# Second GEMM of blocks 1 to 7: units 4 to 6 as seven half-size products, unit 7 added in PSUM

## The chip, the cores and the metric

The kernel runs on one core of a Trainium2 chip. The metric is the device time of one execution in microseconds (us); of several runs the median is given. Trace times count from the span's start. TensorE is PE, VectorE DVE, ScalarE ACT, GpSimd POOL and SyncE SP.

## The reference, cut to what matters

`x` is (4, 1024, 1024). A gate with two decaying scans over the sequence (forward and backward) makes the input of a feed-forward layer, whose result is added to `x`:

```python
num = nf + nb - ekv + euk * vf
den = df + db - ek + euk
base = jax.nn.sigmoid(r) * (num / jnp.maximum(den, 1e-08))
out = base * (0.8 + 0.2 * tf)
...
h = jnp.einsum('bsd,fd->bsf', out, W1)              # W1: 4096 x 1024
q = jnp.clip(jnp.round(h / 0.1), -2**15, 2**15 - 1)
a = jax.nn.gelu(q * 0.1)
x = x + jnp.einsum('bsf,df->bsd', a, W2)            # W2: 1024 x 4096
```

The weights are ternary times powers of two. The kernel checks that they fit its short form (`bad`, the "checks") and has a general path behind a flag, which does not run here.

## The kernel before, in words

The sequence is cut into 8 blocks of 512 positions (`T`), two for each batch entry. For each block 8 tiles of 128 channels are made by the scans (`part`, `newton`, `mixed_out` on DVE; `tile_group` on ACT, exponentials and logarithms). While block n is in the two GEMMs, the tiles of block n+1 are made: `mix(t, p)` is step p of tile t (0 weigh, 1 forward, 2 backward, 3 sums). Where block n+1 is the first half of its batch entry, each tile also needs a prefix over the other half ("late" tiles: two more exponentials on ACT, two more products on DVE). That is so while blocks 1, 3 and 5 are in the GEMMs. Block 7 has no tiles beside it.

Values are split into a high and a low f16 half, and each matmul is done for both. The first GEMM of blocks 1 to 7 has 8 units of 512 hidden channels. Each is done by the seven-product scheme for a 2 x 2 matrix of quadrants: seven products of half the size in both directions instead of eight (`products_15`, `products_73`, `products_26`, `product_4`, L831 to L866), each 16 matmuls of 256 columns, with sums of operands made beforehand (`convert`) and sums of results made in PSUM: `seed` copies product 1 on ACT, `spill_p5` saves product 5 on ACT, `seed_u4` adds on DVE, `quantise22` finishes the fourth quadrant on DVE. The quantised unit goes through GELU on ACT (`gelu`).

In the second GEMM units 0 to 3 are done by the same scheme: `quad_sums` and `quads_lo_*` on DVE and `quads_hi_*` on ACT make the seven operands of a unit, and two output parts e = 0, 1 of four output tiles follow (`y_15_begin`, `y_15_end`, `y_26`, `y_15`, `y_73`, `y_4`, L868 to L929), 32 matmuls of 256 columns for each product. Their quadrants are written out by `y_quad` (ACT) and `y22` (DVE) and added to the output in DRAM by POOL's accumulating DMAs. Units 4 to 7 are done plainly: `act_hi` (ACT) and `act_lo` (DVE) make two halves, and `output` (L947) adds 32 matmuls of 512 columns for each of the 8 output tiles; `output_out` (ACT) empties them. They lie at the end of a block. The last tile of the last block is done in two halves (`output_end`), read back from the output, added and stored (`residual_end`, `result_end`, `store_end`).

The order on each engine is written by hand, block by block: `chained_block` on ACT (L1320) and DVE (L1943), `ffn_block` on SP (L589), the loop at L987 on PE. Every engine works strictly in that order and waits on semaphores. Weights come through a ring of 8 slots filled by SP (`ring_load`, L468); a slot is loaded again when the product that read it is done. A check loads a piece of weights (`load_check`, SP), rounds it to 8 bits (`check_i8`, ACT) and compares (`check`, DVE), with one buffer; a block has eight of them, the last block sixteen. An activation table is loaded whenever ACT changes from exponentials to GELU and back (`tile_group_between`, L1124).

Of the kernel before, what the change touches and what calls it, by code (L numbers as in the profile page):

```python
# [5 lines left out]
P = 128  # L6
# [13 lines left out]
MIX_SCALE = 4.0  # L20
# [18 lines left out]
def adaln_ffn_kernel(nc, x, fside, cond, w, u, w1, w2, out):  # L39
# [18 lines left out]
    CHAIN = STEPS + 2  # L58
# [3 lines left out]
    with ExitStack() as ctx:  # L62
# [11 lines left out]
        w2s = nc.dram_tensor("w2s", [2, P, 4, 2, KH2 * P], F16).ap()  # L74
        w1_quads = w1_half.rearrange("s p (h f k q) -> s p h f k q", h=2, f=2, k=2)
# [5 lines left out]
        wy_ring = w_ring[:, :, :].rearrange("p s (i g m) -> p s i g m", i=2, g=KH2)  # L81
        w_gen = w_ring[:, :, :].bitcast(F32).rearrange("p (s a) n -> p s (a n)", s=2)
# [5 lines left out]
        ao = act_flat[:, 0:SPLIT * 7 * 2 * T].rearrange("p (s o j a t) -> p s o j a t", s=SPLIT, o=7, j=2, a=2)  # L88
# [36 lines left out]
        chk_full = tt_flat[:, 2 * T:4 * T]  # L125
# [6 lines left out]
        chk_i8 = q16[:, 1, 0, :].bitcast(I8)  # L132
        end_full = m_st[:, 0, :, :].rearrange("p k t -> p (k t)")
        end_i8 = m_st[:, 2, 0, 0:T // 2].bitcast(I8)
# [34 lines left out]
        y_end = [halves[7][:, 0, :], halves[2][:, 1, :]]  # L169
# [83 lines left out]
        s_chkload = sem("s_chkload")  # L253
# [12 lines left out]
        s_ev = sem("s_ev")  # L266
        s_yend = sem("s_yend")
        s_resend = sem("s_resend")
# [21 lines left out]
        def part_y(n, e):  # L290

            return CHAIN * (n - 1) + SPLIT + 1 + e

        def emptied(q, c):

            m, r = q // CHAIN, q % CHAIN
            if r in (SPLIT + 1, SPLIT + 2):
                return (s_y11, s_y12, s_y21)[c], 2 * m + r - SPLIT
            return (s_q11, s_q12, s_q21)[c], STEPS * m + (r if r <= SPLIT else r - 2) + 1

        def lo_half(n, s, h):

            return 2 * s + h if n == 0 else 2 * STEPS + 2 * (STEPS - SPLIT) * (n - 1) + 2 * (s - SPLIT) + h

        def quad_unit(n, s):

            return SPLIT * (n - 1) + s

        def act_at(n, s):

            if n == 0:
                return FPS * s
            return FT - FPS if s == SPLIT else FPS * (s - SPLIT - 1)

        def q_at(s, k, h):

            return q_quads[:, s % 2, k, h, :, :] if s < SPLIT else q16[:, s % 2, 2 * k:2 * k + 2, H * h:H * h + H]

        def ao_two(s, o, p):

            return ao[:, s, o:o + 2, :, p, :].rearrange("p o j t -> p (o j) t")

        def w1_pair(s, h):

            return (s // 2 + 2 * h, s % 2) if s < SPLIT else (s, h)
# [7 lines left out]
        def quad(dram, e, c):  # L333

            return dram[4 * e + c // 2:4 * e + 4:2, :, H * (c % 2):H * (c % 2 + 1)].rearrange("i p t -> p i t")

        def event(e, c):

            return ((0, 0), (0, 3), (0, 1), (1, 0), (0, 2), (1, 3), (1, 1), (1, 2)).index((e, c))
# [5 lines left out]
        def buffer_free(engine, n, i):  # L345

            if added(n, i) > 0:
                engine.wait_ge(s_acc[i % 4], 16 * added(n, i))
            elif i % 4 < 2:
                engine.wait_ge(s_res[i % 4], DT // 2)  # L350
            else:
                engine.wait_ge(s_store[i % 4 - 2], 16 * DT // 2)
# [7 lines left out]
        def check_buffers(at):  # L360

            return (chk_full, chk_i8) if at < END_CHECKS else (end_full, end_i8)
# [12 lines left out]
        def y_all(n, d):  # L375

            return y_half(d, 1) if n == 0 else 2 * DT + DT * (n - 1) + d + 1
# [4 lines left out]
        def ring_chunks():  # L382
# [13 lines left out]
            ready_y = [(s_w2store[k], 16 * 4) for k in range(2)]  # L396
            for n in range(1, BLOCKS):
# [14 lines left out]
                def plain(e, r, u, done):  # L412
                    return (w2_half[4 * e + r:4 * e + 4:2, :, u * KH2 * P:(u + 1) * KH2 * P].rearrange("i p n -> p i n"), SLOT,
                            [], [(done, part_y(n, e) + 1)])

                def summed(e, form, done):
                    return (w2s[e][:, form, :, :], SLOT, ready_y if n == 1 and e == 0 and form == 0 else [],
                            [(done, part_y(n, e) + 1)])

# [30 lines left out]
                yield w2_part(0, 1), SLOT, [], [(s_y, y_all(n, 0))]  # L450
                yield h73(LAST)
                yield w2_part(1, 1), SLOT, [], [(s_y, y_all(n, 1))]
                yield h4(LAST)
                for d in range(2, DT):
                    yield w2_part(d, 1), SLOT, [], [(s_y, y_all(n, d))]
# [4 lines left out]
        def _(sp):  # L460
# [7 lines left out]
            def ring_load(times=1):  # L468
                for _ in range(times):
# [45 lines left out]
            def residual_end(n, d):  # L515

                for k in range(4):
                    sp.wait_ge(s_acc[k], 16 * added(n, 8))
                sp.wait_ge(s_acc[1], 16 * (added(n, 2 * DT - 3) + 1))
                sp.dma_start(x_in[:, 1, :], out[n // 2, 1 - n % 2, d]).then_inc(s_x[1], 16)  # L520

            def store_end(n, d):
                sp.wait_ge(s_resend, 1)
                sp.dma_start(out[n // 2, 1 - n % 2, d][:, 0:H], y_out[:, 1, 0:H]).then_inc(s_store[1], 16)
                sp.wait_ge(s_res[1], uses_of(n, d) + 1)
# [1671 lines left out]
```

## Time and profile before

| | us |
|---|---|
| median of 3 runs (1728.91 to 1730.32) | 1729.12 |
| the profiled execution | 1728.37 |
| its span | 1726.6 |
| PE busy | 1648.9 (96%) |
| DVE busy | 1232.5 (71%) |
| ACT busy | 986.4 (57%) |
| POOL busy | 139.2 (8%) |
| mean granted TensorE clock | 0.990 |

Busy times are sums of instructions, and the share is of the span. An instruction can start before the one ahead of it on its engine has ended, so the distance of two starts (the pitch) is often shorter than a duration. In the list of instructions each line has its start, its length, engine, line of the kernel, operation, the tile written and the tiles read, and in brackets the idle time before it with what ended it.

### The profile page before, as it was taken

The numbers are of one execution on the slowest core, as the hardware profiler recorded it, in microseconds if no ns is written. First come the engines' busy times: TensorE is split into PE (matmuls) and PEld (weight loads), VectorE is DVE, ScalarE is ACT, GpSimd is POOL, SyncE is SP. The second block draws the span as 40 slices with busy tenths as digits, with TensorE's granted clock in tenths as the row PEclk, the third lists the DMA queues.
The fourth block names the chain that finished last, engine by engine and source line by source line (L and its number), as shares of the span: only waits on it lengthen the run. The fifth ranks groups of instructions, "written<-read, shape, count | busy, mean of one in ns | idle before, by whom it ended". The sixth has DMA issues, their size and how long they took to land. (4 is left out here: it accounts for less than half of the span.)

```text
span 1726.6 us, 30636 instructions
## 1 busy us (share of the span) xinstructions
PE 1648.9 (96%) x12258; PEld 1199.1 (69%) x12258; DVE 1232.5 (71%) x1684; ACT 986.4 (57%) x1558; POOL 139.2 (8%) x155
## 2 busy tenths in 40 slices
PE   1699999999999999999999999999999999999996
PEld 0234445888578884888658885688847887488863
DVE  8888797878768658687677767786886875854131
ACT  4577423765666565674747656476666647465341
POOL 0000110011000101002010010001010010100101
PEclk9799999999999999999999999999999999999998
DMA  8979895688575866769386684868757694676754
GB/s 237 237 183 275 276 333 172 218 254 220 127 244 188 252 177 183 237 200 262 122 218 236 214 232 127 235 215 248 226 137 217 204 247 151 175 243 200 195 185 98
DMA packets 131205, 362.54 MB, mean 210 GB/s; under 512 B 14000, under 2 KB 28592, under 8 KB 130096
## 3 DMA queue, kind: packets, MB, share of 16 engines
q1 hardware_dynamic: 105216, 308.33, 52.8%
q0 software_dynamic: 25840, 52.18, 17.8%
q8 instruction: 99, 1.62, 0.4%
q14 instruction: 50, 0.41, 0.1%
HBM read 333.19 MB, written 81.79 MB: 240 GB/s over the span
## 5 line engine op out<-in xcount | busy, mean ns | idle before, releaser
L813 PE MATMUL ps<-mo,w_ring 128*128 128x256 f16 x6272 | 695.1, 273 | 5.1 <-DVE q L1758 2.7
L813 PEld LDWEIGHTS ps<-mo,w_ring 128*128 128x128 f16 x6272 | 613.1, 98 | 82.5 <-issue 7.1
L957 PE MATMUL ps<-act,w_ring 128*128 128x512 f16 x1760 | 383.3, 379 | 0.0
L876 PE MATMUL ps<-act,w_ring 128*128 128x256 f16 x3136 | 348.1, 273 | 0.7
L876 PEld LDWEIGHTS ps<-act,w_ring 128*128 128x128 f16 x3136 | 305.8, 98 | 38.4 <-issue 2.5
L957 PEld LDWEIGHTS ps<-act,w_ring 128*128 128x128 f16 x1760 | 172.2, 98 | 203.2
L1784 DVE SCALAR_TENSOR_TENSOR act<-a,act 128x1024 f16<-128x1024 f32 x72 | 87.8, 1222 | 91.3 <-ACT act L1233 91.3
L1223 ACT ACTIVATE a<-q 128x1024 f32<-128x1024 int16 x124 | 131.0, 1057 | 7.0 <-DVE act L1784 2.0
L724 POOL DMA_DIRECT2D out_dram<-xy x56 | 66.9, 1195 | 810.6 <-ACT xy L1257 709.6
L1746 DVE SCALAR_TENSOR_TENSOR ps<-sp,ps 128x512 f32<-128x512 f32 x70 | 48.4, 692 | 110.2 <-issue 49.4
L754 PE MATMUL ps<-mo,w_ring 128*128 128x512 f16 x256 | 66.7, 424 | 56.8 <-DMA w_ring<-w_half 34.9
L943 PE MATMUL ps<-act,w_ring 128*128 128x512 f16 x512 | 110.7, 379 | 0.0
L1273 ACT ACTIVATE q<-tt 128x1024 int8<-128x1024 f32 x48 | 50.4, 1049 | 77.0 <-DMA tt<-in_w_dram 77.0
L754 PEld LDWEIGHTS ps<-mo,w_ring 128*128 128x128 f16 x256 | 26.5, 107 | 96.4 <-issue 47.4
L943 PEld LDWEIGHTS ps<-act,w_ring 128*128 128x128 f16 x512 | 50.1, 98 | 60.4
L729 POOL DMA_DIRECT2D out_dram<-xy x55 | 47.6, 883 | 544.1 <-ACT xy L1264 539.0
L1257 ACT ACTIVATE xy<-ps 128x512 f32<-128x512 f32 x42 | 24.7, 588 | 112.0 <-PE ps L876 112.0
L1648 DVE SCALAR_TENSOR_TENSOR ND<-EE,bonus,ND 128x1024 f32<-128x1024 f32 x64 | 81.9, 1280 | 2.9
L1845 DVE SCALAR_TENSOR_TENSOR tt<-q,tt 128x1024 f32<-128x1024 int8 x48 | 58.6, 1221 | 35.0 <-ACT q L1273 34.9
L1628 DVE TENSOR_TENSOR_SCAN ND<-decay,back,ND 128x512 f32<-128x512 f32 x64 | 81.9, 1280 | 0.6
L1632 DVE TENSOR_TENSOR_SCAN ND<-decay,back,ND 128x512 f32<-128x512 f32 x64 | 81.6, 1276 | 0.0
L1172 ACT ACTIVATE ps<-ps 128x512 f32<-128x512 f32 x70 | 40.8, 582 | 68.4 <-PE ps L813 38.2
(132 smaller groups left out, 1812.0 us busy)
## 6 DMA issues: line engine op xcount, KB each, us to landing
w_ring<-w1s SPq DMA_DIRECT2D x168, 512.0 KB, 5.7
w_ring<-w_half SPq DMA_DIRECT2D x130, 512.0 KB, 5.5
w_ring<-w2s SPq DMA_DIRECT2D x56, 512.0 KB, 5.1
out_dram<-xy POOLq DMA_DIRECT2D x111, 256.0 KB, 6.2
tt<-in_w_dram SPq DMA_DIRECT2D x48, 512.0 KB, 5.3
V<-in_fside_dram SPq DMA_DIRECT2D x64, 256.0 KB, 5.6
R<-in_x_dram SPq DMA_DIRECT2D x64, 256.0 KB, 5.9
w_half<-in_w_dram POOLq DMA_DIRECT2D x16, 1024.0 KB, 10.3
```

Of the source, the lines that this page charges most:

```text
L724: pool.dma_start(quad(dram, e, c), xy_quads[:, k, :, :], accum_op=ALU.add).then_inc(s_acc[k], 16)
L754: mm = pe.matmul(bank[4 * (s % 2) + j][:, :], w1_ring[:, slots[2 * s + j // 2], j % 2, c, :], mix0[:, c, p, :], start=(first and p == 0), ...
L813: mm = pe.matmul(dst[:, f, :], wp_ring[:, k, r, f, q, :], mo[:, op, q, p, :], start=(fresh and f == 0 and q == 0 and p == 0), stop=(q == K ...
L876: mm = pe.matmul(dst[:, i, :], wy_ring[:, k, i, 2 * s + j, :], ao[:, s, op, j, p, :], start=(fresh and i == 0 and s == 0 and j == 0 and p ...
L943: mm = pe.matmul(y_ps[y][:, :], w2_ring[:, k, f, :], act[:, FPS * s + j, p, :], start=(h == 0 and f == 0 and p == 0), stop=(h == 1 and f = ...
L957: mm = pe.matmul(bank[d][:, :], w2_ring[:, k, FPS * (s - SPLIT) + j, :], act[:, act_at(n, s) + j, p, :], start=(s == SPLIT and j == 0 and ...
L1223: sc.activation(a32[:, 2 * h:2 * h + 2, :], src[:, s % 2, 2 * h:2 * h + 2, :], ACT.Gelu_apprx_tanh, scale=QSTEP).then_inc(s_gelu, 1)
L1628: v.tensor_tensor_scan(DEN[:, k, :][:, ::-1], dec(b, c), DEN[:, k, :][:, ::-1], back[:, k, 1:2], ALU.mult, ALU.add).then_inc(s_dbwd, 1)
L1632: v.tensor_tensor_scan(NUM[:, k, :][:, ::-1], dec(b, c), NUM[:, k, :][:, ::-1], back[:, k, 0:1], ALU.mult, ALU.add).then_inc(s_nbwd, 1)
L1648: v.scalar_tensor_tensor(out=ND[:, k, :, :], in0=EE[:, k, :, :], scalar=bonus[:, b, c:c + 1], in1=ND[:, k, :, :], op0=ALU.mult, op1=ALU.ad ...
L1784: v.scalar_tensor_tensor(out=act[:, f:f + 2, 1, :], in0=a32[:, 2 * h:2 * h + 2, :], scalar=ACT_SCALE, in1=act[:, f:f + 2, 0, :], op0=ALU.m ...
L1845: v.scalar_tensor_tensor(out=full, in0=small, scalar=1.0 / W_SCALE, in1=full, op0=ALU.mult, op1=ALU.not_equal, accum_out=bad[:, at:at + 1] ...
```

## The change

Units 4 to 6 also go through the seven-product scheme in the second GEMM, as two further output parts e = 2, 3, with 24 matmuls of 256 columns for each product. Unit 7 keeps its two plain halves and is added to the quadrants of these parts in PSUM by `z_product`: 16 matmuls of 256 columns for each quadrant; the fourth quadrant goes on top of product 5 in its bank, which is then spilled again (`spill_z`). `output`, `output_out` and `output_end` go. The operands of units 4 to 6 take the place of operands that are done with (`operand_at`).

The weight sums for the new products (`w2f`) are made in block 1: `f_load` and `f_store` are DMAs issued by ACT, `f_sums` is on DVE. POOL copies unit 7's weights together once (`w2z`). The weights of the new parts come in 14 pieces of 384 KB and two of 512 KB for each block where eight of 512 KB came.

The checks have two buffers at each place and their loads are issued by ACT (`check_load`, `next_check`) and not by SP. The output's last quadrant is read back early into a buffer of its own.

The diff is long; this is its core. First the new functions and the order on PE:

```diff
+            def z_product(n, k, dst, c):
+
+                r, h = c // 2, c % 2
+                for i in range(2):
+                    for j in range(FPS):
+                        pe.wait_ge(s_alo, lo_half(n, LAST, j // 2) + 1)
+                        for p in range(2):
+                            mm = pe.matmul(dst[:, i, :], wz_ring[:, k, 2 * i + r, j, :],
+                                           act[:, act_at(n, LAST) + j, p, h * H:(h + 1) * H],
+                                           start=False, stop=(j == FPS - 1 and p == 1), skip_group_check=True)
+                return mm
...
+                begun = y_15_begin(n, 2)
                 products_73(n, LAST)
...
+                y_15_end(n, 2, begun)
+                y_26(n, 2)
                 product_4(n, LAST)
...
+                y_15(n, 3)
+                y_73(n, 2)
+                held = loaded()
+                z_22(n, 2, held)
+                z_11(n, 2, held)
+                z_12(n, 2, held)
+                y_26(n, 3)
+                y_4_end(n, 2, held)
+                held = loaded()
+                z_22(n, 3, held)
+                y_73(n, 3)
+                z_11(n, 3, held)
+                z_12(n, 3, held)
+                y_4_end(n, 3, held)
...
+            def spill_z(n, e):
+
+                q = part_y(n, e)
+                act_e.wait_ge(s_z22, 2 * (n - 1) + e - 1)
+                act_e.wait_ge(s_u4, q + 1)
+                act_e.wait_ge(s_sp5, q + 1)
+                sc.activation(sp5[:, q % 2, :], bank[4 * (q % 2) + 2][:, :], ACT.Copy, scale=1.0 / MIX_SCALE).then_inc(s_zsp, 1)
...
+            def f_load(k):
+
+                if k == 0:
+                    block_done(act_e, 0)
+                else:
+                    act_e.wait_ge(s_fsum, 4 * k)
...
+            def check_load(at):
+
                 if at > 0:
...
+                    act_e.wait_ge(s_chk, at - 1)
...
+                act_e.dma_start(check_buffers(at)[0], check_rows(at)).then_inc(s_chkload[at % 2], 16)
+
+            def next_check(*ats):
+
+                for at in ats:
+                    if at % DT in (1, 2, 5, 6) if at < END_CHECKS else END_CHECKS < at < 2 * STEPS * FPS - 1:
+                        check_load(at + 1)
+                    check_i8(at)
...
+            def f_sums(k):
+
+                dve.wait_ge(s_fload, 32 * (k + 1))
...
+                upper, lower = f_in[:, 0, :, :], f_in[:, 1, :, :]
+                v.tensor_tensor(f_out[:, 0, :], lower[:, 0, :], lower[:, 1, :], ALU.add).then_inc(s_fsum, 1)
```

The order on ACT from unit 6's product 5 on, and in block 1 (lines taken out are left away):

```diff
+                    if n == 1 and s > 2:
+                        f_store(s - 3)
+                        f_load(s - 2)
...
                 seed(hid(n, SPLIT + 2))
                 spill_p5(hid(n, SPLIT + 2))
                 if nxt:
                     tile_group(g0 + 5)
+                    next_check(at + 3)
+                    check_load(at + 4)
+                    check_load(at + 5)
...
                 quantise12(n, SPLIT + 1)
                 gelu(n, SPLIT + 1, 0)
                 quantise11(n, SPLIT + 2)
...
+                quads_hi_11(n, SPLIT + 1)
                 quantise21(n, SPLIT + 1)
                 gelu(n, SPLIT + 1, 1)
                 seed(hid(n, LAST))
...
+                quads_hi_2(n, SPLIT + 1)
                 spill_p5(hid(n, LAST))
...
+                quads_hi_t(n, SPLIT + 1)
+                if nxt:
+                    tile_group_between(g0 + 6)
+                else:
+                    next_check(at + 10)
                 quantise12(n, SPLIT + 2)
                 gelu(n, SPLIT + 2, 0)
                 quantise11(n, LAST)
...
+                quads_hi_11(n, SPLIT + 2)
                 quantise21(n, SPLIT + 2)
                 gelu(n, SPLIT + 2, 1)
...
+                quads_hi_2(n, SPLIT + 2)
+                quads_hi_t(n, SPLIT + 2)
+                quantise12(n, LAST)
+                seed(part_y(n, 2))
```

The order on DVE from output part 0 on (likewise):

```diff
+                if n == 1:
+                    f_sums(3)
                 seed_u4(part_y(n, 0))
                 mix(2, 0, 1)
...
+                quads(SPLIT)
                 mix(2, 2)
...
+                y22(n, 0)
                 mix(2, 3)
...
                 mix(3, 0, 1)
...
+                seed_u4(part_y(n, 1))
+                mix(3, 2, 3)
+                check(at if nxt else at + 7)
+                mix(4, 0)
+                y22(n, 1)
+                if nxt:
+                    check(at + 1)
+                mix(4, 1, 2)
+                seed_u4(hid(n, SPLIT + 1))
+                mix(4, 3)
+                if nxt:
+                    check(at + 2)
+                mix(5, 0, 1)
+                quantise22(n, SPLIT + 1)
+                check(at + 3 if nxt else at + 8)
+                mix(5, 2)
+                seed_u4(hid(n, SPLIT + 2))
+                mix(5, 3)
+                quads(SPLIT + 1)
                 quantise22(n, SPLIT + 2)
...
+                mix(6, 0)
                 seed_u4(hid(n, LAST))
...
+                quads(SPLIT + 2)
+                mix(6, 1)
+                quantise22(n, LAST)
+                mix(6, 2)
+                act_lo(n, LAST, 0)
+                check(at + 4 if nxt else at + 11)
+                seed_u4(part_y(n, 2))
+                mix(6, 3)
+                act_lo(n, LAST, 1)
...
+                convert(n + 1, 0)
                 mix(7, 0)
...
+                convert(n + 1, 1)
                 mix(7, 1)
...
+                y22(n, 2)
+                mix(7, 2)
+                check(at + 5)
+                seed_u4(part_y(n, 3))
```

## Rows read from the trace of the kernel before

**Rows 1.** The page, part 1: busy time, share of the span, instructions.

```profile
PE 1648.9 (96%) x12258; PEld 1199.1 (69%) x12258; DVE 1232.5 (71%) x1684; ACT 986.4 (57%) x1558; POOL 139.2 (8%) x155
```

**Rows 2.** Five blocks: length, busy PE, PEld, DVE, ACT, POOL (instructions), PEclk, DMA, GB/s.

```profile
289.06:491.30 202.24, 202.13 (x1601) 156.42 (x1600) 155.84 (x217) 126.96 (x201) 15.59 (x15) 1.00 0.70 205
491.30:693.77 202.47, 202.30 (x1602) 156.34 (x1600) 145.71 (x185) 122.76 (x192) 16.14 (x16) 1.00 0.69 204
693.77:898.10 204.33, 202.46 (x1602) 156.25 (x1601) 158.62 (x225) 129.43 (x204) 15.96 (x17) 1.00 0.70 210
898.10:1102.54 204.44, 202.45 (x1601) 156.27 (x1600) 147.38 (x189) 122.77 (x192) 17.31 (x17) 1.00 0.69 203
...
1508.92:1711.40 202.48, 202.37 (x1633) 159.42 (x1631) 71.79 (x104) 91.46 (x117) 15.54 (x16) 1.00 0.64 191
```

**Rows 3.** Instructions of PE in order of time, block 3 (start, length, idle before).

```profile
720.98 3.65 PE L813 MATMUL ps<-mo,w_ring 128*128 128x256 f16 x32 [0.85 <-ACT ps L1172]
725.55 26.36 PE L813 MATMUL ps<-mo,w_ring 128*128 128x256 f16 x240 [0.92 <-DVE q L1758]
...
770.96 24.62 PE L876 MATMUL ps<-act,w_ring 128*128 128x256 f16 x224
...
849.75 48.51 PE L957 MATMUL ps<-act,w_ring 128*128 128x512 f16 x224
```

**Rows 4.** DMA issues by line: KB each, median us from issue to landing.

```profile
tt<-in_w_dram SPq DMA_DIRECT2D x48, 512.0 KB, 5.3
```

**Rows 5.** Instructions in order of time at the span's end, PE and DVE.

```profile
1704.26 7.15 PE L973 MATMUL ps<-act,w_ring 128*128 128x256 f16 x64
...
1719.93 0.42 DVE L1833 SCALAR_TENSOR_TENSOR xy<-ps,xy 128x256 f32<-128x256 f32 x1 [8.20 <-DMA xy<-out_dram]
```

**Rows 6.** Instructions of DVE in order of time, block 3.

```profile
727.59 0.68 DVE L1573 SCALAR_TENSOR_TENSOR EE<-EKP,EE 128x512 f32<-128x512 f32 x1
...
737.46 1.28 DVE L1608 TENSOR_TENSOR_SCAN ND<-decay,pre_n,EE 128x512 f32<-128x512 f32 x1
...
740.54 0.69 DVE L1746 SCALAR_TENSOR_TENSOR ps<-sp,ps 128x512 f32<-128x512 f32 x1
741.44 1.23 DVE L1795 TENSOR_TENSOR tt<-a 128x1024 f32<-128x1024 f32 x1 [0.21 <-ACT a L1223]
...
748.64 1.28 DVE L1628 TENSOR_TENSOR_SCAN ND<-decay,back,ND 128x512 f32<-128x512 f32 x1
...
752.33 0.69 DVE L1746 SCALAR_TENSOR_TENSOR ps<-sp,ps 128x512 f32<-128x512 f32 x1
...
780.25 1.22 DVE L1845 SCALAR_TENSOR_TENSOR tt<-q,tt 128x1024 f32<-128x1024 int8 x1
...
781.39 1.28 DVE L1648 SCALAR_TENSOR_TENSOR ND<-EE,bonus,ND 128x1024 f32<-128x1024 f32 x1
...
783.32 0.68 DVE L1767 SCALAR_TENSOR_TENSOR xy<-ps,sp 128x512 f32<-128x512 f32 x1
```

**Rows 7.** Instructions of ACT in order of time, a tile group of block 3.

```profile
840.60 1.28 ACT L1126 ACT_TABLE_LOAD   x1
...
843.04 0.71 ACT L1095 ACTIVATE EE<-RAMP,lndec 128x512 f32<-128x512 f32 x1
...
846.89 1.28 ACT L1223 ACT_TABLE_LOAD   x1
```

**Rows 8.** Instructions of DVE in order of time, block 1 (it starts at 289.06).

```profile
322.41 0.69 DVE L1746 SCALAR_TENSOR_TENSOR ps<-sp,ps 128x512 f32<-128x512 f32 x1
```

**Rows 9.** Instructions of SP's queue in order of time, two issues in block 3.

```profile
769.88 0.41 SPq L536 DMA_DIRECT2D tt<-in_w_dram  x1
770.34 0.43 SPq L490 DMA_DIRECT2D VP<-in_fside_dram  x1
```

**Rows 10.** Instructions of PE in order of time, block 0.

```profile
71.29 23.77 PE L754 MATMUL ps<-mo,w_ring 128*128 128x512 f16 x96 [6.28 <-DVE mo L1675]
```

**Rows 11.** Busy time by stretch, block 0 (columns as in rows 2).

```profile
71.00:83.00 12.00, 11.71 (x41) 4.74 (x42) 11.18 (x17) 8.14 (x17) 0.49 (x1) 0.74 0.80 198
```

More of the change, by code:

```diff
@@ L252, in adaln_ffn_kernel @@
         s_store = [sem(f"s_store{k}") for k in range(2)]
-        s_chkload = sem("s_chkload")
+        s_chkload = [sem(f"s_chkload{k}") for k in range(2)]
         s_chki8 = sem("s_chki8")
@@ L265, in adaln_ffn_kernel @@
         s_acc = [sem(f"s_acc{k}") for k in range(4)]
-        s_ev = sem("s_ev")
-        s_yend = sem("s_yend")
-        s_resend = sem("s_resend")
+        s_z22 = sem("s_z22")
+        s_zsp = sem("s_zsp")
+        s_w2z = sem("s_w2z")
+        s_fload = sem("s_fload")
+        s_fsum = sem("s_fsum")
+        s_fstore = [sem(f"s_fstore{k}") for k in range(2)]
         s_vote = sem("s_vote")
@@ L396, in ring_chunks @@
             ready_y = [(s_w2store[k], 16 * 4) for k in range(2)]
+            ready_f = [(s_fstore[k], 16 * 4) for k in range(2)]
             for n in range(1, BLOCKS):
@@ L708, in _ @@
                 pool.dma_start(w2_half[d], w2_full[d]).then_inc(s_w2cast[d], 16)
+            for d in range(DT):
+                pool.wait_ge(s_w2cast[d], 16)
+            for e in range(2):
+                for u in range(2):
+                    rows = w2_half[4 * e:4 * e + 4].rearrange("d p (u n) -> d p u n", u=4)[:, :, 2 + u, KF * P:KH2 * P]
+                    pool.dma_start(w2z[e][:, :, u, :], rows.rearrange("d p n -> p d n")).then_inc(s_w2z, 16)
             for s in range(STEPS):
@@ L1988, in chained_block @@
-                seed_u4(part_y(n, 1))
-                mix(3, 2)
-                mix(3, 3)
-                y22(n, 1)
-                mix(4, 0)
-                mix(4, 1)
-                seed_u4(hid(n, SPLIT + 1))
-                mix(4, 2)
-                if not nxt:
-                    check(at + 5)
-                mix(4, 3)
-                quantise22(n, SPLIT + 1)
-                mix(5, 0)
-                seed_u4(hid(n, SPLIT + 2))
-                act_lo(n, SPLIT + 1, 0)
-                mix(5, 1)
@@ L2048, in chained_block @@
-                if nxt:
-                    convert(n + 1, 3)
-                    check(at + 5)
+                y22(n, 2)
+                mix(7, 2)
+                check(at + 5)
+                seed_u4(part_y(n, 3))
+                mix(7, 3)
+                convert(n + 1, 2)
+                y22(n, 3)
+                divide(g0 + 7)
+                convert(n + 1, 3)
                 if n + 2 < BLOCKS:
```

686 lines of the change are left out of this document (355 added, 331 removed).

## The prediction

> **What bounds the kernel now.** I began with the page's first line and then took the busy times block by block. TensorE is busy 96% of the span [rows 1], and in blocks 1 to 7 it is busy 202.1 to 202.5 us of blocks that last 202.2 to 204.4 us [rows 2]. A matmul that is not waiting is therefore the bound, and the reader should first see what one costs. In block 3, 224 matmuls of 512 columns begin at 849.75 and the block ends 48.35 us later, so one takes 215.8 ns; 224 of 256 columns take 24.46 us (24.62 less the 0.16 by which a line's last matmul outlasts its pitch), so one takes 109.2 ns [rows 3]. The only waits of TensorE in that block are 0.85 us for ScalarE's seed and 0.92 us for VectorE's `quantise22` [rows 3]; they are why blocks 3, 4 and 5 are about 1.8 us longer than the others [rows 2] (block 5 reads like block 3 with 203.9 us, block 6 like block 2 with 202.5; of the seven rows five stand). The second thing to see is what cover is left: VectorE is busy 156 to 159 us in blocks 1, 3 and 5, where the tiles of the next block carry a prefix, about 146 us in blocks 2, 4 and 6, and 72 us in block 7, which has no tiles [rows 2].
>
> **TensorE's own gain.** A block loses 8 x 4 x 4 x 2 = 256 matmuls of 512 columns (55.3 us). It gains 2 x 7 x 24 = 336 of 256 columns for units 4 to 6 and 2 x 4 x 16 = 128 for unit 7, 464 in all (50.7 us). That is 4.6 us a block and 32.2 us in seven, all of it on the path. The last block's 64 half-width matmuls already stand for 32 wide ones, so it saves the same.
>
> **The waits of blocks 3 to 5.** They come from ScalarE sitting on a check's load, of which there was one buffer: a load takes 5.3 us to land [rows 4], and the check before it must be done first. With two buffers the load for the start of a block is issued in the block before or one check ahead. I take the 1.8 us in three blocks as gone, 5.3 us.
>
> **The end.** TensorE's last long line ends at 1711.4 and the span at 1726.6. VectorE waited 8.20 us there for a read-back of the output, and from its result at 1719.93 to the end are 6.7 us [rows 5]. Afterwards the read-back lies early, and the result follows the last matmul at once: 0.1 us, the 6.7, 0.3 for a result of twice the size and up to 3 for a store of twice the bytes, 10.1 us against 15.2, so 5 less. Without any new wait the time would be 1728.4 - 32.2 - 5.3 - 5 = 1685.9 us, taking the profiled execution's own 1728.37 us (span 1726.6; the median of the three runs, 1729.12, lies 0.04% above).
>
> **What the other engines get.** One unit in seven products costs VectorE 6.6 us: from its first sum at 741.44 to the backward scan at 748.64 are 7.2 us, of which 0.6 is a `quantise22` [rows 6]. Two `act_lo` go, of 1024 elements like the check that starts at 780.25, whose pitch is 1.14 us [rows 6]. Three units add 13 us, two `seed_u4` and two `y22` 2.4 us: VectorE comes to 174 us of 197.8 in a late block, 161 in an early one. ScalarE gains about 7 us: four stores instead of two per unit, and two seeds, four spills and six quadrants instead of eight outputs. Neither becomes the bound by its sum. What counts is the order, because the stretch that goes, 48 us of plain matmuls that waited for nobody, was where both engines caught up.
>
> **Late blocks (1, 3, 5), in order of time from the block's start.** Positions of TensorE are counts of matmuls times 109.2 ns. The pieces of VectorE are pitches of rows 6: weigh 2.07 us (three operations of 0.69 from 727.59), forward 3.08 (737.46 to 740.54), backward 3.69 (748.64 to 752.33), check 1.14, sums 1.93 (781.39 to 783.32).
> (a) Unit 5. The spill of unit 6's fifth product can't come before matmul 1104, at 120.5 us. Behind it in ScalarE's order stands the tile group, whose weight is ready 1.87 us after the group's first operation (841.88, behind the table load, to 843.75) [rows 7], so with the spill's 0.6 at 123.0. VectorE must weigh and scan before `quantise22` of unit 5: 123.0 + 2.07 + 3.08 + 0.7 = 128.9. TensorE wants that at matmul 1168, 127.5 us: 1.5 us late.
> (b) Unit 6. Check, backward, seed, sums, seven-product sums and `quantise22`: 128.9 + 1.14 + 3.69 + 0.6 + 1.93 + 6.6 + 0.7 = 143.6. TensorE stands there at 141.4: 2.3 us.
> (c) The fifth product of output part 2 needs unit 6's sums. ScalarE was held until check `at + 3` is done (the load of `at + 5` waits for it) and reaches the tile group at 140.2. A group between two GELUs takes 5.7 us (840.60 to 846.89, less the 0.6 of a quantise) and the way back a table load of 1.28 us [rows 7], so the GELU ends at 151.4, and sums, stores and lower halves take 5.6 us more: 157.0 against 153.1: 3.9 us.
> (d) `y22` of part 2 stands behind two conversions and a scan: 187.6 against 185.9: 1.7 us.
> The four come to 9.4 us. In blocks 3 and 5 the tile group ahead of the block's last quadrant delays the first seed, and the start costs 1.1 us more: 10.5 us.
>
> **Early blocks (2, 4, 6).** Weighing is one operation (0.6 us) and the group lacks two exponentials (1.15 us). (a) and (d) fall within the margin, (b) leaves 0.9 and (c) 2.6 us: 3.5 us.
>
> **Block 1's weight sums.** VectorE gets four times four sums on 128x768 f16, a form no row has; the nearest row, 512 f32 elements, takes 0.69 us [rows 6], and between half of that and all of it I take 0.5, 2 us a group. `seed_u4` of unit 2 ended 0.9 us before TensorE wanted it (322.41 + 0.69 is 34.0 us into the block, and the third product starts at 34.9) [rows 8], so the first group costs about 1.9 us with the issues ahead of it. The second and third wait for loads that ScalarE issues some 45 and 61 us into the block and that land 5.3 us later, behind a VectorE that is ready sooner: 2.9 and 1.6, and 0.5 at unit 3's sums. That is 6.9 us on top of (a) to (d), 16.3 in all. Bounds: 0 if the loads are early, 11 if every issue holds ScalarE.
>
> **Block 7's checks.** Sixteen checks in pairs, each second load issued only when the pair before is done, ahead of `seed_u4`: ScalarE sits on a landing of 5.3 us in units 3 and 4. I get 3.2 and 1.3 us, 1.1 at unit 3's sums and 1.9 at unit 6's: 7.5 us.
>
> **DMAs issued by ScalarE.** Eight check loads a block leave the SP queue for ScalarE's. SP's issues stand 0.46 us apart [rows 9]; whether one holds ScalarE as long, no row shows, so between 0 and 0.46. I take half, since the sequencer can issue beside a running activation of 0.6 to 1 us; it is in the sums above. [...] Loads of tiles and weights stay ahead: the tail's weights grow from 4.2 to 6.6 MB a block at 0.70 busy DMA [rows 2], and eight slots reach some 20 us ahead.
>
> **Sum.** 16.3 + 2 x 10.5 + 3 x 3.5 + 7.5 = 55.3 us of new waits. 1685.9 + 55.3 = 1741.2, so 1741 us. The work saved is real; the waits cost more.
>
> **Rivals.** (B) Faster: the lateness of (a) and (b) isn't there. Both are differences of one to two per cent of 130 us of in-order work, so if VectorE reaches `quantise22` of unit 5 by 127.4 us, (a) and (b) vanish and (c), fed by the same chain, halves: 5.7 us less in each late and 2.2 in each early block, 23.7 in all: 1717 us. For it speaks that VectorE's 174 us leave 23 us in a late block; against it, that the weight exponential is bound to a spill, not to VectorE's load. (C) Slower still: TensorE's clock falls in the longest waits. After a wait of 6.28 us, 96 matmuls took 23.77 us instead of 20.72, and the granted clock over 71 to 83 us was 0.74, between the two levels of 1.2 and 2.4 GHz [rows 10, 11]; after waits of 0.9 us in block 3 the clock stays at 1.00 [rows 2, 3]. Four waits of 3 to 4 us at up to 3.05 us each give 1753. [...] (D) Gains and waits cancel: within 0.2% (3.5 us, about what a measurement of this kernel can tell from no change) of 1729, if 40 to 47 us of waits remain.
>
> **Chances and range.** The forecast 0.46 (its own range 1733 to 1748), B 0.34, C 0.10, D 0.10. Faster is B, 0.34; same is D, 0.10; slower 0.56. From B's lower side, where block 1's and block 7's waits shrink too, to C's upper: 1702 to 1758.
>
> **What would show it.** Right: blocks of about 198 us busy PE; a late block near 208 us, an early one near 201, block 1 longest at 214; PE waits named for `quantise22`, for the lower halves at the fifth product of part 2, and for `seed_u4` in block 1. The 0.85 and 0.92 us waits gone; some 10 us behind the last matmul. Wrong: late blocks under 202 us, or loads, not VectorE and ScalarE, as releasers.

## The result and the profile after

The changed kernel takes 1763.13 us (median; 1762.53 to 1767.07) where the kernel before takes 1729.01 us: ratio 1.0204, 95% interval 1.0188 to 1.0221. It is slower, as forecast, but by 34 us where 12 were predicted, and 5 us outside the range. The profiled execution took 1763.2 us, its span is 1761.4 us.

The first line is the page's line of busy times (of before: [rows 1]); below it stand stretches of the changed kernel, columns as in [rows 2]: blocks 1, 2, 3 and 7, and what follows the last matmul. Blocks 5 and 4, 6 read like 3 and 2 (208.2, 205.0 and 205.0 us).

```profile
PE 1637.3 (93%) x13682; PEld 1342.7 (76%) x13682; DVE 1343.2 (76%) x1839; ACT 1028.5 (58%) x1635; POOL 162.2 (9%) x159
```

```profile
288.44:518.24 229.80, 205.11 (x1809) 178.29 (x1808) 178.19 (x253) 133.25 (x212) 17.57 (x15) 0.97 0.70 215
518.24:723.43 205.19, 199.84 (x1810) 177.10 (x1808) 161.94 (x208) 128.95 (x204) 20.09 (x17) 0.99 0.73 214
723.43:931.38 207.95, 200.21 (x1811) 176.96 (x1808) 172.50 (x241) 135.60 (x215) 18.76 (x16) 0.99 0.72 216
...
1549.50:1754.30 204.80, 199.80 (x1810) 176.96 (x1807) 87.56 (x125) 97.24 (x128) 19.34 (x16) 0.99 0.73 208
1754.30:1761.40 7.10, 0.24 (x4) 0.09 (x2) 0.74 (x2) 0.00 (x0) 0.00 (x0) 0.87 0.28 69
```

Three things are to be read here. A block has 1808 matmuls of 256 columns; at the 109.2 ns of [rows 3] they are 197.4 us, so the work saved is there. Over the 197.8 us that the prediction's sum gives a block without waits, blocks 1 to 7 are 32.0, 7.4, 10.2, 7.2, 10.3, 7.2 and 7.0 us longer, 81.3 in all, where 16.3, 3.5, 10.5, 3.5, 10.5, 3.5 and 7.5, 55.3 in all, were forecast. So the miss lies in block 1 (16 us) and in the early blocks (4 us each). And TensorE's busy time is above 197.4 us in every block while its granted clock is below 1: part of the loss is no wait.

The waits of TensorE, over the whole span (engine, line, tile, releaser: us in total, times, longest). The first line is block 0, where the kernel before waits likewise.

```profile
PE ps L783 <- DVE mo L1803: 56.2, 6, 34.0
PE ps L842 <- DVE q L1886: 15.4, 12, 2.0
PE ps L842 <- DVE ps L1874: 14.9, 5, 7.5
PE ps L905 <- DMA w_ring<-w_half: 14.7, 7, 2.3
PE ps L905 <- DVE act L1953: 8.6, 7, 1.2
PE ps L905 <- DVE act L1935: 4.3, 7, 0.9
PE ps L905 <- issue: 2.2, 1, 2.2
PE ps L905 <- DVE ps L1874: 0.8, 1, 0.8
```

L842 is `product`, L905 `y_product` and L918 `z_product`; L1886 is `quantise22`, L1874 `seed_u4`, L1935 and L1953 are unit 6's conversions. The line `issue` is `y22` of output part 0 in block 1: its row on VectorE ends at 404.84 and TensorE goes on at 404.95. It and the last line (`seed_u4` of part 1 in block 1) are not in the prediction, but VectorE comes to them late from block 1's weight sums, which are in it; both waits are gone in the run with earlier loads for these sums. The load of a weight chunk is in no step of it: 2.0 to 2.3 us in each of the seven blocks. From the second line on the waits are 60.9 us. Some 15.6 us more are matmuls at a lower clock: 5.5 in block 1, 1.7 in each other block (in blocks 2, 4, 6 and 7, for instance, a line of 72 matmuls takes 9.70 us instead of 8.03). The rest is about what 40 waits give at the 0.16 us by which a line's last matmul outlasts its pitch.

**The load.** Block 2 of the changed kernel, SP's queue, TensorE and the granted clock (last column but two) behind the wait:

```profile
672.84 0.47 SPq L553 DMA_DIRECT2D w_ring<-w2z  x1
693.40 0.36 SPq L553 DMA_DIRECT2D w_ring<-w_half  x1
```

```profile
689.71 5.40 PE L918 MATMUL ps<-act,w_ring 128*128 128x256 f16 x48
697.30 9.70 PE L905 MATMUL ps<-act,w_ring 128*128 128x256 f16 x72 [2.18 <-DMA w_ring<-w_half]
```

```profile
697.00:700.00 3.00, 2.70 (x16) 2.08 (x17) 3.00 (x6) 1.21 (x3) 0.00 (x0) 0.66 1.05 341
700.00:703.00 3.00, 3.00 (x23) 2.41 (x22) 3.00 (x4) 0.00 (x0) 2.58 (x3) 0.77 1.01 386
```

SP stands still for 20 us between two issues. What it waits for is in the diff: `plain_f(2, 0, 1, s_p2)` gives its slot back with `s_p2`. For parts 0 and 1 `y_26` signals `s_p2` when it has read the chunk; for parts 2 and 3 it does not, and `z_11` signals it when unit 7's quadrant 11 is done. TensorE has read the chunk at 674.9 (32 matmuls of 109.2 ns after 671.36), some 18 us earlier. `z_11` is the second of the three products of 16 that begin at 689.71, so it ends at 693.2; SP issues at 693.40, and TensorE, which goes from `z_12` straight to the product that reads this chunk, waits for the landing. Behind the wait the granted clock is 0.66 and 0.77, between its two levels of 1.2 and 2.4 GHz.

**Block 1.** ScalarE's queue, VectorE and TensorE; L1339 is `f_load`, L1969 the first of a group of sums:

```profile
332.05 1.87 ACTq L1339 DMA_DIRECT2D act<-w_half  x2
...
342.63 0.56 DVE L1969 TENSOR_TENSOR xy<-act 128x768 f16<-128x768 f16 x1 [6.95 <-DMA act<-w_half]
...
345.47 11.00 PE L842 MATMUL ps<-mo,w_ring 128*128 128x256 f16 x80 [7.53 <-DVE ps L1874]
```

```profile
DMA to landing us min/median/max: 4.4/7.7/12.3
```

The sums of this pair of loads begin 10.6 us after the first issue, not 5.3; for the next two pairs it is 8.8 and 12.9 us. The last line is the landing of the eight loads, each from its own issue.

**A late block.** VectorE, ScalarE and TensorE in block 3, which begins at 723.43:

```profile
847.22 0.69 DVE L1701 SCALAR_TENSOR_TENSOR EE<-EKP,EE 128x512 f32<-128x512 f32 x1 [2.19 <-ACT EE L1138]
...
852.57 0.68 DVE L1886 SCALAR_TENSOR_TENSOR q<-ps,sp 128x512 int16<-128x512 f32 x1
...
867.12 0.68 DVE L1886 SCALAR_TENSOR_TENSOR q<-ps,sp 128x512 int16<-128x512 f32 x1
...
875.56 1.23 DVE L1927 TENSOR_TENSOR tt<-a 128x1024 f32<-128x1024 f32 x1 [5.08 <-ACT a L1265]
```

```profile
854.81 0.60 ACT L1240 ACTIVATE q<-ps 128x512 int16<-128x512 f32 x1 [4.15 <-DVE tt L2000]
```

```profile
853.40 12.58 PE L842 MATMUL ps<-mo,w_ring 128*128 128x256 f16 x112 [1.67 <-DVE q L1886]
867.95 2.94 PE L842 MATMUL ps<-mo,w_ring 128*128 128x256 f16 x16 [1.96 <-DVE q L1886]
...
878.90 1.05 PE L905 MATMUL ps<-act,w_ring 128*128 128x256 f16 x8 [0.38 <-DVE act L1935]
881.17 6.29 PE L905 MATMUL ps<-act,w_ring 128*128 128x256 f16 x56 [1.22 <-DVE act L1953]
```

This is the chain of steps (a) to (c): the weight exponential behind the spill (VectorE idle 2.19 us), `quantise22` of unit 5 at 129.1 us into the block (128.9 forecast at its end), ScalarE held 4.15 us by the check, `quantise22` of unit 6 at 143.7 (143.6 forecast), unit 6's GELU at its end only 152.1 (151.4 forecast).

### The profile page after: what moved, and what is told of

Its sections match the earlier page's. It is cut to its first block and busy times, and to the rows that moved or that the text cites. A ratio compares the mean times of both kernels' runs of the same rounds, so it can differ in the third digit from the quotient of the medians.

```text
span 1761.4 us, 34209 instructions
## 1 busy us (share of the span) xinstructions
PE 1637.3 (93%) x13682; PEld 1342.7 (76%) x13682; DVE 1343.2 (76%) x1839; ACT 1028.5 (58%) x1635; POOL 162.2 (9%) x159
## 5 line engine op out<-in xcount | busy, mean ns | idle before, releaser
L842 PE MATMUL ps<-mo,w_ring 128*128 128x256 f16 x6272 | 703.9, 274 | 30.4 <-DVE q L1886 15.4
L842 PEld LDWEIGHTS ps<-mo,w_ring 128*128 128x128 f16 x6272 | 614.2, 98 | 110.7 <-issue 36.0
L905 PE MATMUL ps<-act,w_ring 128*128 128x256 f16 x5488 | 622.4, 275 | 30.6 <-DMA w_ring<-w_half 14.7
L905 PEld LDWEIGHTS ps<-act,w_ring 128*128 128x128 f16 x5488 | 538.7, 99 | 104.7 <-DMA w_ring<-w_half 16.7
L757 POOL DMA_DIRECT2D out_dram<-xy x111 | 134.6, 1355 | 1375.0 <-ACT xy L1321 798.5
L1874 DVE SCALAR_TENSOR_TENSOR ps<-sp,ps 128x512 f32<-128x512 f32 x84 | 58.1, 692 | 117.9 <-PE ps L842 61.7
L1927 DVE TENSOR_TENSOR tt<-a 128x1024 f32<-128x1024 f32 x49 | 59.9, 1223 | 90.4 <-ACT a L1265 90.4
L1953 DVE SCALAR_TENSOR_TENSOR act<-tt,act 128x1024 f16<-128x1024 f32 x91 | 107.4, 1218 | 5.2 <-ACT act L1304 5.2
L1012 PE MATMUL ps<-act,w_ring 128*128 128x512 f16 x512 | 110.7, 380 | 0.0
L1321 ACT ACTIVATE xy<-ps 128x512 f32<-128x512 f32 x83 | 47.1, 589 | 95.6 <-PE ps L905 66.0
L918 PE MATMUL ps<-act,w_ring 128*128 128x256 f16 x896 | 102.4, 273 | 0.0
L1012 PEld LDWEIGHTS ps<-act,w_ring 128*128 128x128 f16 x512 | 50.0, 98 | 60.5
L918 PEld LDWEIGHTS ps<-act,w_ring 128*128 128x128 f16 x896 | 87.6, 98 | 10.2
L1189 ACT ACTIVATE mo<-tt 128x1024 f16<-128x1024 f32 x28 | 29.5, 1055 | 97.5 <-DVE tt L1818 97.5
L1246 ACT ACTIVATE q<-ps 128x512 int16<-128x512 f32 x56 | 33.2, 593 | 83.2 <-PE ps L842 77.3
```

The lines of the kernel that those rows point to most:

```text
L757: pool.dma_start(quad(dram, e, c), xy_quads[:, k, :, :], accum_op=ALU.add).then_inc(s_acc[k], 16)
L842: mm = pe.matmul(dst[:, f, :], wp_ring[:, k, r, f, q, :], mo[:, op, q, p, :], start=(fresh and f == 0 and q == 0 and p == 0), stop=(q == K ...
L905: mm = pe.matmul(dst[:, i, :], wy_ring[:, k, i, 2 * (s - base) + j, :], ab[:, operand_at(s, op), j, p, :], start=(fresh and i == 0 and s = ...
L918: mm = pe.matmul(dst[:, i, :], wz_ring[:, k, 2 * i + r, j, :], act[:, act_at(n, LAST) + j, p, h * H:(h + 1) * H], start=False, stop=(j == ...
L1012: mm = pe.matmul(y_ps[y][:, :], w2_ring[:, k, f, :], act[:, FPS * s + j, p, :], start=(h == 0 and f == 0 and p == 0), stop=(h == 1 and f = ...
L1927: v.tensor_tensor(tq[:, 0:2, :], a_quads[:, :, 1, :], a_quads[:, 0, :, :], ALU.subtract).then_inc(s_gt, 1)
```

## Experiments

They ran on four chips, where the kernel before takes 1725.5 to 1727.3 us, so ratios to it are compared; 0.1% is 1.7 us, and the changed kernel stands at 1.0204. An interval is mostly 0.0017 to each side, so the difference of two ratios is known to some 4 us.

**The slot.**

```diff
-                yield plain_f(2, 0, 1, s_p2)
+                yield plain_f(2, 0, 1, s_p6)
...
-                yield plain_f(3, 0, 1, s_p2)
+                yield plain_f(3, 0, 1, s_p6)
```

> Only the release of one weight slot changes: the two lower-row weight chunks of parts 2 and 3 are given back after the sixth product of their part (s_p6) and no longer after the first quadrant of unit 7 (s_p2, which those parts signal some 15 us later). Theory, the slot: the load that TensorE waits for in front of the second product of part 3 (2.0 to 2.3 us in each of blocks 1 to 7) is late only because SP holds it until that quadrant is done; the seven waits go (14.7 us), and with them the clock loss of 1.7 us behind them in blocks 2, 4, 6 and 7 (6.7 us): 1763 - 21 = 1742 us. Rival, the DMA: the busy share is 1.0 to 1.2 in that stretch, so an earlier load lands little earlier, at least 1 us of each wait stays: 1755 us or more.

Ratio 1.0114 (1.0098 to 1.0131): 15.5 us gained of 21. Block 2, SP's queue and TensorE, then three lines of TensorE in block 3:

```profile
676.29 0.36 SPq L553 DMA_DIRECT2D w_ring<-w_half  x1
...
693.56 8.02 PE L905 MATMUL ps<-act,w_ring 128*128 128x256 f16 x72
```

```profile
862.53 1.91 PE L842 MATMUL ps<-mo,w_ring 128*128 128x256 f16 x16 [1.96 <-DVE q L1886]
873.48 1.17 PE L905 MATMUL ps<-act,w_ring 128*128 128x256 f16 x8 [2.06 <-DVE act L1935]
875.75 8.88 PE L905 MATMUL ps<-act,w_ring 128*128 128x256 f16 x56 [1.10 <-DVE act L1953]
```

SP issues some 16 us sooner in the block and the seven waits are gone: the slot, not the DMA. The rest of the expected gain went into the late blocks: there the 16 matmuls run at full clock now, so TensorE comes sooner to unit 6's conversions and waits 2.06 us instead of 0.38, and the clock falls behind that wait (56 matmuls in 8.88 us instead of 6.29). Block 3 takes 208.4 us there, beside 208.0 in the changed kernel. So the clock loss of 1.7 us ahead of that wait had cost nothing by itself: in the changed kernel it took the place of part of (c).

**The loads of the weight sums.**

```diff
                     spill_p5(hid(n, s))
+                    if n == 1 and s > 2:
+                        f_store(s - 3)
+                        f_load(s - 2)
                     quads_hi_t(n, s - 2)
...
-                    if n == 1 and s > 2:
-                        f_store(s - 3)
-                        f_load(s - 2)
...
+                if n == 1:
+                    f_store(2)
+                    f_load(3)
                 quantise21(n, SPLIT - 1)
...
                 seed(part_y(n, 0))
-                if n == 1:
-                    f_store(2)
-                    f_load(3)
```

> Only in block 1: each store and each next load of the sums of the second half's weights is issued by ScalarE one place earlier, right behind the spill of the fifth product (the last pair before the quantise21 of unit 3), some 7 us sooner. Theory, the issue: VectorE's idle 7.0, 6.7 and 11.2 us ahead of the second to fourth group of sums are the landing of a load that ScalarE issues too late; the waits of 7.5 and 4.0 us of TensorE for seed_u4 and the 3.8 us of lower clock behind them go down to 1 to 2 us in all: 1763 - 14 = 1749 us. Rival, the landing: a pair of these loads takes 9 to 10 us among the other loads of block 1, so that it is late wherever it is issued: less than half of that is gained, 1756 us or more.

Ratio 1.0140 (1.0123 to 1.0157): 11 us gained of 14. TensorE in block 1, then ScalarE's `quantise21` of unit 3:

```profile
337.12 8.89 PE L842 MATMUL ps<-mo,w_ring 128*128 128x256 f16 x80 [0.48 <-DVE ps L1874]
356.93 1.05 PE L905 MATMUL ps<-act,w_ring 128*128 128x256 f16 x8 [2.18 <-DVE act L1935]
```

```profile
351.87 0.60 ACT L1246 ACTIVATE q<-ps 128x512 int16<-128x512 f32 x1 [6.64 <-issue]
```

The wait of 7.53 us is 0.48, that of 4.02 is gone: the place of the issue decides, since a landing still takes 4.4 to 9.1 us, median 7.1 instead of 7.7. Missing are 3.4 us of new waits ahead of part 0 (2.18 and 1.22): the third store and the fourth load, which had stood behind the seed of part 0, now stood ahead of `quantise21` of unit 3, and ScalarE stood idle for 6.64 us there.

**`quantise22` ahead.**

```diff
-                mix(5, 0, 1)
                 quantise22(n, SPLIT + 1)
+                mix(5, 0, 1)
...
-                quads(SPLIT + 1)
                 quantise22(n, SPLIT + 2)
+                quads(SPLIT + 1)
```

> Only VectorE's order changes, in blocks 1 to 6: quantise22 of unit 5 stands ahead of the weighing and forward scan of tile 5, quantise22 of unit 6 ahead of the sums of unit 5. Theory, one chain: the waits of 1.7 and 2.0 us in late blocks and 1.0 us in early ones go, but VectorE and ScalarE reach unit 6's sums no sooner, so TensorE waits as much more for unit 6's lower halves ahead of part 2; only some clock loss comes back: 1759 to 1765 us. Rival, separate waits: what is gained stays gained, 3 x (1.67 + 1.96 + 1.7 of clock) + 3 x 1.0 = 19 us: 1744 us.

Ratio 1.0309 (1.0287 to 1.0332), 18 us slower: both theories missed. VectorE and TensorE in block 4:

```profile
1061.16 0.69 DVE L1886 SCALAR_TENSOR_TENSOR q<-ps,sp 128x512 int16<-128x512 f32 x1 [2.88 <-PE ps L842]
1073.39 0.69 DVE L1886 SCALAR_TENSOR_TENSOR q<-ps,sp 128x512 int16<-128x512 f32 x1 [0.63 <-PE ps L842]
...
1091.24 1.05 PE L905 MATMUL ps<-act,w_ring 128*128 128x256 f16 x8 [3.91 <-DVE act L1935]
```

`quantise22` now stands ahead of its own product: VectorE, in order, waits 2.88 and 0.63 us for TensorE with tile 5 and unit 5's sums queued behind, and unit 6's conversions come that much later; TensorE waits 3.91 and 1.22 us there instead of 1.00 for `quantise22`, 0.94 and 1.22. Over the span the waits for `quantise22` fall from 15.4 to 0.9 us, and those for the first of unit 6's conversions (L1935) rise from 4.3 to 28.0. So the waits are one chain, as the theory said, but I had not asked when TensorE has the product ready.

**Unit 6's conversions.** (`stored` and the wait of `gelu` on `s_glo` follow the new order.)

```diff
-                quads(SPLIT + 2)
+                quads_lo_11(n, SPLIT + 2)
+                quad_sums(n, SPLIT + 2)
+                quads_lo_t(n, SPLIT + 2, 0)
+                quads_lo_2(n, SPLIT + 2)
+                quads_lo_t(n, SPLIT + 2, 1)
```

> Only the order of unit 6's conversions on VectorE changes: the lower half of quadrant 11 first, then the sums, then the lower halves of T1 and T3, and only then those of the quadrants 21 and 22. Theory, the order: the waits ahead of part 2's first and fifth product (0.38 + 1.22 us late, 0.94 + 1.22 early, 0.34 + 1.22 in block 7) go, 13 us in all: 1750 us. Rival: the seed of part 2 or quantise22 of unit 7 is next in line within 0.5 us and takes their place: 1757 us or more.

Ratio 1.0128 (1.0111 to 1.0145): 13.1 us gained, as the theory has it. Late blocks wait no more ahead of part 2, early ones 0.6 us.

**Together.** The three edits, with the third store and fourth load behind unit 3's conversions and `f_sums` behind `seed_u4`:

> The three edits that helped, together: the earlier slot release, the earlier loads for the weight sums (the third store and load now behind the conversions of unit 3, where they held ScalarE before quantise21, and the sums on VectorE behind seed_u4 instead of ahead of it), the new order of unit 6's conversions. Theory, separate places: the gains add, 15 + 11 + 12 us and 2 more for the place of the third load, so the changed kernel's 2.04% above the kernel before turn into 0.2% below it. Rival, one chain: part 2 comes sooner, so the waits go over to unit 6's conversions and the clock falls there; half of the sum is left, 1% above the kernel before.

Ratio 0.9984 (0.9974 to 0.9993): the gains of 15.5, 11.0 and 13.1 us (39.6) add up within the noise (38 us, where the theory had 40). Three changes of place outweigh the whole loss of 35 us.

**The exponentials.** `exps` is split, and ScalarE issues its first part where it stood idle:

```diff
                     next_check(at + 2)
+                    exps_head(g0 + 5)
                 y_quad(n, 1, 2)
...
-                    tile_group(g0 + 5)
+                    tile_group(g0 + 5, False)
                     next_check(at + 3)
+                    exps_head(g0 + 6)
...
-                    tile_group_between(g0 + 6)
+                    tile_group_between(g0 + 6, False)
```

> The changed kernel with one edit on ScalarE: the first exponentials of tiles 5 and 6 (prefix, tile, weight) are issued earlier, those of tile 5 ahead of quadrant 21 of part 1, where ScalarE stood idle 3.0 us, those of tile 6 behind the check at + 3, where it stood idle 4.2 us. Theory, the chain: the late weight exponential sets the waits of late blocks (VectorE idle 2.19 us for it); quantise22 of unit 5 comes 2.2 us earlier and its wait of 1.67 us goes, unit 6's lower halves come some 4 us earlier, and the clock loss of 1.7 us goes too: 4 to 5 us in each of blocks 1, 3 and 5, up to 1 us in the early ones: 14 us faster than the changed kernel, 1.2% above the kernel before. Rival, VectorE full: it has no idle time between these steps but that one, other work fills it, and the wait only moves to quantise22 of unit 6: within 4 us of the changed kernel.

Ratio 1.0093 (1.0077 to 1.0110): 19 us faster than the changed kernel, where 14 were expected. VectorE and TensorE in block 3:

```profile
838.97 0.69 DVE L1711 SCALAR_TENSOR_TENSOR EE<-EKP,EE 128x512 f32<-128x512 f32 x1
```

```profile
835.11 22.87 PE L842 MATMUL ps<-mo,w_ring 128*128 128x256 f16 x208
859.70 1.91 PE L842 MATMUL ps<-mo,w_ring 128*128 128x256 f16 x16 [1.72 <-DVE q L1896]
```

VectorE no longer idles for the weight, and TensorE runs through where it waited 1.67 us for `quantise22` of unit 5. It is the prediction's cause of (a), the exponential bound to a spill, not VectorE's load. Block 1 keeps its 1.86 us. The waits beyond block 0 are 13.1 us less; the rest is clock, which here stayed up behind the load waits of blocks 2, 6 and 7 (8.03 us for the 72 matmuls).

**Unit 6 on VectorE, with and without them.** On top of the three edits, `quantise22` of unit 6 between unit 5's conversions and unit 3's conversions in unit 6's order; then that kernel with the early exponentials:

> The run of three edits with two more on VectorE: unit 3's conversions in the new order, and quantise22 of unit 6 between unit 5's conversions instead of behind them (2.35 us sooner). Theory, one chain: the waits of 2.0 us late and 1.0 us early for it go, but the lower halves of unit 6 come no sooner, so part 2 waits for them: within 4 us of the run of three edits. Rival, separate: 3 x 2.0 + 3 x 1.0 us and the clock loss behind them stay gained, 14 us faster than the run of three edits, 1.0% below the kernel before.

> All edits together: three edits, unit 3's order, quantise22 of unit 6 between unit 5's conversions, and the early exponentials. Theory: with the exponentials early the chain up to unit 6 is some 4 us shorter in late blocks, so that the waits for quantise22 go and only 1 to 2 us a block are left at part 2: 15 to 20 us faster than the run of three edits, 1.1% below the kernel before. Rival, VectorE full: as fast as the run of three edits, within 5 us.

Ratios 0.9977 (0.9966 to 0.9989) and 0.9909 (0.9893 to 0.9926). The first gains 1 us on the run of three: the wait for `quantise22` of unit 6 goes and comes back, in late blocks as 3.65 us for unit 6's conversions. The second gains 11.7 us on the first and 12.9 on the run of three, less than the 15 to 20 of its theory. Where the waits are one chain, only work at its head counts.

**What was late next.** `y22` of part 2 ahead of tile 7's forward scan (`mix(7, 1)`); then also block 1's fourth load behind the seed of part 0; then also the check and `seed_u4` of part 3 ahead of `mix(7, 2)`:

> The run of all edits with one more on VectorE: y22 of part 2 ahead of the forward scan of tile 7 instead of behind it (3.1 us sooner). Theory, step (d) of the prediction: TensorE's wait ahead of the seventh product of part 2 (2.6 us in blocks 1 and 3, 0.6 to 1.0 in the others) is for y22 of part 2, and it goes, with the clock loss of 1.7 us behind it in blocks 1 and 3: 12 us faster than the run of all edits, 1.6% below the kernel before. Rival, the spill: y22 waits for ScalarE's spill of part 2 and not for the scan, so VectorE only idles and the tiles fall behind: no gain.

> As the run with y22 of part 2 early, and in block 1 the third store and fourth load of the weight sums behind the seed of part 0 again, since ScalarE holds that seed while it issues them (TensorE waits 1.8 us there). Theory: 1.8 us less than that run; rival: the fourth group of sums comes later and holds quantise22 of unit 4 or part 0: no gain or 2 us more.

> As the last run (all edits, y22 of part 2 early, the seed of part 0 ahead of the fourth load), with the check and seed_u4 of part 3 ahead of the backward scan of tile 7 as well. Theory, one queue: the wait of 2.1 us ahead of the seventh product of part 3 in blocks 3 and 5 (0.2 to 0.5 in others) goes, and the clock loss of 1.7 us behind it: 8 us less than that run, 1.7% below the kernel before. Rival: the tiles fall behind by as much, and the next block's start waits: no gain.

Ratios 0.9874, 0.9869 and 0.9828 (0.9812 to 0.9845). Block 3 of the kernel without (TensorE, VectorE) and with the first of these edits (TensorE):

```profile
879.55 4.45 PE L905 MATMUL ps<-act,w_ring 128*128 128x256 f16 x24 [2.63 <-issue]
...
878.76 0.69 DVE L1907 SCALAR_TENSOR_TENSOR xy<-ps,sp 128x512 f32<-128x512 f32 x1
```

```profile
886.40 7.07 PE L905 MATMUL ps<-act,w_ring 128*128 128x256 f16 x48 [2.12 <-DVE ps L1884]
```

The wait of 2.63 us ends with `y22`, so it is step (d); moved ahead, it hands 2.12 us on to `seed_u4` of part 3 and half of the gain is lost (6 us of 12); the last edit brings that too. The edit between gained 1 us of 1.8, not clear of noise. The last kernel takes 1696.94 us beside 1727.25 for the kernel before, 1.7% less. Its waits of TensorE beyond block 0:

```profile
PE ps L905 <- DVE act L1963: 7.0, 4, 2.1
PE ps L842 <- ACT ps L1223: 3.1, 3, 1.0
PE ps L842 <- DVE q L1896: 2.8, 3, 1.9
PE ps L842 <- DVE ps L1884: 1.5, 2, 1.2
```

**The slot once more.** The last kernel with only the slot's release put back:

> The kernel of the run beside it with one edit undone: the two lower-row weight chunks of parts 2 and 3 are again given back only after unit 7's quadrant. Theory, the slot priced by itself: seven load waits of 2.0 to 2.3 us come back, 14.7 us, and 1.7 us of lower clock behind those where the clock has not just fallen, at most 12 us: 15 to 26 us slower than the kernel beside it. Rival: with the other waits gone the slot is hidden behind other waits of TensorE: under 7 us.

Ratio 0.9933 (0.9916 to 0.9950): 18 us slower (17.4 by the two medians, 1714.31 and 1696.94 us on one chip), within the theory's range. Two of its blocks, TensorE and the clock behind the wait:

```profile
671.31 9.70 PE L905 MATMUL ps<-act,w_ring 128*128 128x256 f16 x72 [2.05 <-DMA w_ring<-w_half]
...
875.29 8.03 PE L905 MATMUL ps<-act,w_ring 128*128 128x256 f16 x72 [2.04 <-DMA w_ring<-w_half]
```

```profile
671.30:674.30 3.00, 2.99 (x18) 2.20 (x19) 3.00 (x5) 2.10 (x4) 1.59 (x3) 0.62 1.06 360
875.30:878.30 3.00, 3.00 (x28) 2.69 (x29) 2.81 (x5) 3.00 (x5) 0.00 (x0) 1.00 1.05 384
```

The seven waits are 14.1 us, and three blocks of seven lose 1.67 us of clock besides: one semaphore's name is worth 17 to 18 us.

## Why the prediction was wrong

The direction was right: the work is saved, and new waits are larger than the saving. The size was wrong, and in part the mechanism: the prediction named loads as releasers as a sign of being wrong, and loads end 14.7 us of the 60.9. The profiled execution lies 22 us above the sum. Load waits of 14.7 us, a lower clock of 15.6 and 9.8 us more of waits in block 1 are 40 us that the sum did not have; (c), (d), the start, block 7's checks and the end came out 22 us under their terms, and the 0.16 us at each wait make up most of the rest. Its steps in turn:

- **TensorE's own gain, DVE's and ScalarE's loads.** Right: 197.4 us of matmuls a block; VectorE 172.5 us late and 161.9 early (174 and 161 forecast).
- **(a) and (b).** Right: 1.67 us for 1.5, 1.96 for 2.3, in early blocks nothing and 1.00 for 0.9. Rival B, VectorE in time, falls; that the weight exponential is the head of the chain is shown by the run that issues it earlier.
- **(c).** Too large: 1.6 us for 3.9 late, 2.2 for 2.6 early. The converted halves came when forecast (unit 6's GELU within 0.7 us); TensorE came later, by 0.5 us of the start and 1.7 us of clock.
- **(d) and the start.** (d) lay under the load wait and showed as 2.6 us in late blocks once that was gone, in the run of three edits (1.7 forecast). The start costs 0.47 us, not 1.1.
- **Late blocks** came out at 10.2 and 10.3 us for 10.5 by luck: 2.0 us of load and 1.7 us of clock that weren't in the sum stand for what (c), (d) and the start had too much. In early blocks only 0.4 us of (c) stand against them, hence 7.2 for 3.5.
- **The missed term.** "Loads of tiles and weights stay ahead" is the step that failed. I weighed bytes and slots and did not follow each chunk's release to the instruction that signals it, so the term stood at nothing. The runs showed seven load waits, 14.7 us, and a clock fall behind some of them; the release and its counter-run put the term at 15.5 and 18 us.
- **Block 1's weight sums.** A term mis-sized: 6.9 us forecast with a bound of 11; measured 16.7 us of waits and 3.8 of clock. The 5.3 us to land were those of a single load from SP; a pair takes 8.8 to 12.9 us from its first issue to the sums, and the next pair is issued only when ScalarE's order comes round. The early loads removed 11 us and left 0.48 us of the 7.53.
- **Block 7.** 7.0 us for 7.5, but not by the checks: they cost 1.14 us once. The rest is the load wait, unit 6's conversions and the clock.
- **The end.** 7.1 us behind the last matmul, 10.1 forecast: from the store's issue to the end are 6.1 us (5.8 for the old one), where up to 3 more were allowed. The waits at the start of blocks 3 to 5 fell as forecast, but for 0.47 us in blocks 3 and 5.
- **DMAs issued by ScalarE.** Half of 0.46 us was assumed. A check's load stands mostly 0.33 to 0.35 us in its queue and holds ScalarE only where no activation runs (at 831.02 it lies beside one of 0.63 us, at 854.43 ScalarE stands still for it), so the middle value was fair. The Trainium skill's page "DMA: Bandwidth & Descriptors" (section "Issuing engines are not separate DMA queues") says that the time to start a transfer is usually small beside the transfer; here 0.34 us stands beside median landings of 5.1 to 6.7 us.
- **Rival C** had the right thing in the wrong place: I gave the clock's fall to waits of 3 to 4 us, which no row of the kernel before shows, with a chance of 0.10, and it came at 2 us. Its price of 12 us is near the 15.6 us that the clock took; it belonged into every case as a term, where it would have moved the whole range up.

## What to carry to other kernels

Where a change splits or moves the last reader of a buffer, follow every release to the instruction that signals it: a slot named free by the wrong event costs a landing on the bottleneck engine at each use, and a sum of bytes does not show it. Of waits that hang on one in-order chain only the head is worth moving; a consumer moved further ahead waits for its own producer. And price a load by its landing among the transfers of its own stretch, counted from where its issuing engine's order really puts it.

## What the hardware showed

A wait of 2 us can take TensorE's clock down for the next matmuls, and need not: in the run with the slot's release put back, waits of 2.05 and 2.04 us at the same place of blocks 2 and 3 left it at 0.62 and at 1.00. In all, waits of 1.98 to 2.08 us there were followed by 72 matmuls in 9.70 us in blocks 1, 2 and 6, and waits of 1.94 to 2.05 us by 72 in 8.03 us in the four others. Behind the waits of 0.9 us in the kernel before it stayed at 1.00 [rows 2, 3]. In the kernel with all edits waits of 1.83 to 2.10 us in blocks 1, 3 and 5 left the mean of each block at 1.00. So the length of one wait does not settle it; what does, these runs don't show. The Trainium skill's page "TensorE: Matmul & The Clock Gate" (Part 1) says that idleness takes the clock to the lower level; the 0.62 and 0.66, between the two levels, agree. In the changed kernel a fall cost 1.7 us in blocks 2 to 7; with the slot released early, behind the wait of 2.06 us, it cost 2.6 (56 matmuls in 8.88 us instead of 6.29).
